# A graph-attention layer with gated residual and layernorm: reworked prologue, VectorE's own products in batch 0, x plus one moved on ScalarE

## What is computed

```python
h = einsum('bnd,ade->bane', x, W)            # features, per head
th = tanh(h)
attn = th @ w_src + swapaxes(th @ w_dst)     # 512 x 512 scores per head
attn = leaky_relu(attn, 0.2); attn = where(adj, attn, -999); attn = softmax(attn)
f = elu(concat(attn @ h + b))
gate = sigmoid(x @ H_w.T + H_b)
out = layernorm(x + gate * f + (1 - gate) * x)
```

## Time and profile before

| | us |
|---|---|
| median of 3 runs | 749.0 (747.43 to 750.62) |
| the profiled execution | 748.52 |
| its span | 746.7 |
| PE busy | 684.6 (92%) |
| DVE busy | 691.3 (93%) |
| ACT busy | 377.5 (51%) |
| POOL busy | 596.5 (80%) |

### The profile page before, as it was taken

How to read it: one execution, slowest core, us unless ns; L and a number is a source line. 1 busy time by engine, 2 the same in 40 slices (tenths; PEclk the granted TensorE clock), 3 DMA queues, 4 the chain that set the end, 5 groups by cost and what they waited for, 6 DMA issues and landing times.

```text
span 746.7 us, 12632 instructions
## 1 busy us (share of the span) xinstructions
PE 684.6 (92%) x3411; PEld 395.1 (53%) x3472; DVE 691.3 (93%) x1281; ACT 377.5 (51%) x804; POOL 596.5 (80%) x437
## 2 busy tenths in 40 slices
PE   4399999999999999999999999999999999999970
PEld 4355555555565555656555565655646465563430
DVE  8779999999999999999999999999999999999876
ACT  5123537374564637456473746547274654727161
POOL 6884697998979798897979889797988989793500
PEclk9599999999999999999999999999999999999995
DMA  5300111113121111212111121211211131111102
GB/s 184 99 1 2 57 43 43 58 43 100 44 98 42 45 58 47 89 42 98 42 55 60 51 73 42 98 42 69 64 49 57 42 98 42 57 43 43 42 2 84
DMA packets 32875, 43.82 MB, mean 59 GB/s; under 512 B 1234, under 2 KB 26580, under 8 KB 32852
## 3 DMA queue, kind: packets, MB, share of 16 engines
q1 hardware_dynamic: 24660, 31.35, 13.5%
q10 hardware_dynamic: 8192, 12.19, 4.5%
HBM read 30.95 MB, written 12.58 MB: 58 GB/s over the span
## 4 chain that ended last, share of the span: by engine, by line
PE 72%; DVE 17%; issue 5%; ACT 3%; DMA 2%; DVEq 1%; SPq 0%; POOL 0%; ACTq 0%; POOLq 0%
PE out_T L826 37%; PE hg L750 24%; DVE ew L610 9%; PE tr L834 5%; PE vb L812 4%; DVE ex L645 2%; PE hg L797 1%; DVE sd L559 1%; DMA ew<-in_HwT 1%; DVE th_w L541 1%; ACT x_plus L415 1%; PE hg L802 1%; DVE att L628 1%; ACT h_sb L381 1%; DVE ex L704 1%
## 5 line engine op out<-in xcount | busy, mean ns | idle before, releaser
L610 DVE SCALAR_TENSOR_TENSOR ew<-vb,u,adj_in 128x512 f32<-128x512 f32 x768 | 533.0, 737 | 2.3 <-PE vb L812 2.3
L826 PE MATMUL out_T<-ew,vals 128*64 128x512 f32 x1536 | 360.0, 600 | 3.3 <-DVE ew L610 1.3
L826 PEld LDWEIGHTS out_T<-ew,vals 128*64 128x64 f32 x1536 | 110.0, 136 | 194.5 <-issue 161.3
L258 POOL TENSOR_TENSOR th_w<-th,score_w 128x768 f32<-128x768 f32 x60 | 110.1, 1835 | 67.2 <-ACT th L380 61.6
L410 ACT ACTIVATE att_T<-out_T,tiny 128x512 f32<-128x512 f32 x96 | 66.1, 688 | 163.2 <-PE out_T L826 163.1
L750 PE MATMUL hg<-w_hi,xT_hi 128*128 128x384 f32 x384 | 109.7, 394 | 19.3 <-ACT xT_hi L371 7.7
L750 PE MATMUL hg<-w_hi,xT_lo 128*128 128x384 f32 x384 | 88.6, 338 | 0.3 <-DVE xT_lo L526 0.3
L750 PE MATMUL hg<-w_lo,xT_hi 128*128 128x384 f32 x384 | 88.2, 337 | 0.0
L750 PEld LDWEIGHTS hg<-w_hi,xT_hi 128*128 128x128 f32 x384 | 70.3, 194 | 27.2 <-issue 23.3
L262 POOL TENSOR_TENSOR th_w<-th_w 128x384 f32<-128x384 f32 x60 | 80.2, 1337 | 4.7
L387 ACT ACTIVATE gate_tanh<-hg 128x384 f32<-128x384 f32 x64 | 31.4, 490 | 95.7 <-PE hg L750 95.7
(11 more groups left out here) (97 smaller groups left out, 759.6 us busy)
## 6 DMA issues: line engine op xcount, KB each, us to landing
xT_in<-in_xT SPq DMA_DIRECT2D x16, 768.0 KB, 4.6
x_in<-in_x SPq DMA_DIRECT2D x16, 768.0 KB, 4.5
out<-y ACTq DMA_DIRECT2D x15, 768.0 KB, 3.5
adj_in<-in_adjT SPq DMA_DIRECT2D x16, 256.0 KB, 4.8
ew<-in_W SPq DMA_DIRECT2D x1, 576.0 KB, 4.2
ew<-in_HwT SPq DMA_DIRECT2D x1, 576.0 KB, 8.1
score_w<-in_w_rows SPq DMA_DIRECT2D x1, 384.0 KB, 7.1
out<-y SPq DMA_DIRECT2D x1, 384.0 KB, 2.5
```

The source lines that it names most:

```text
L258: g.tensor_tensor(th_w[:, c % 2], th[:, c].unsqueeze(1).broadcast_to([P, 2, D]), score_w[:], ALU.mult).then_inc(S["thw_done"], 1)
L610: ve.scalar_tensor_tensor(out=ew[:, (2 * C * j + i) % SLOTS, :], in0=VB[h % 4][:], scalar=u[:, q, c, h:h + 1], in1=adj_in[:, q, c, :], op0 ...
L826: te.matmul(OUT[VW * k:VW * k + VW, :], vals[:, q, c, h, :], ew[:, t % SLOTS, :], start=(c == 0), stop=(c == C - 1)).then_inc(S["ew_free"], 1)
```

## The change

- The gate weights are loaded into a buffer of their own. Their high part (ScalarE) is made after `copy_vT(0, 0)`, their low part (VectorE, `gate_low`) within batch 0's second head pair. The gate bias is split by ScalarE and GpSimd instead of VectorE.
- `head_sel` is built as a 12-wide `row_sel` by GpSimd and widened by one ScalarE copy.
- GpSimd adds batch 0's bias only after the column maximum, and makes only two of the four low splits of batch 1 before the values, the other two after the row sums.
- For batch 1, VectorE makes the score products of chunks 0 and 1 itself (`head_products`) and sums them 768 wide; GpSimd weighs only chunks 2 and 3.
- Batch 1's feature blocks alternate between the two banks. ScalarE's copy of a block of batch 1 waits for the values of its chunk and for the row sum, its tanh no longer does. The first attention matmuls wait for the values chunk by chunk.
- TensorE gets 58 matmuls without use for the result (`warm_up`), into the bank TR: 12 before the features, 16 after, 4 and 24 around the maximum's broadcast, 2 before the first `vb`.
- In every step ScalarE does x plus one behind the second feature block instead of in front of the first.

```diff
                 return HG[(c + 1) % 2]
+            if isinstance(b, int) and b == 1:
+                return HG[c % 2]
             return HG[1] if c == 3 else HG[0]
...
                 sp.dma_start(bias_row[:], bias.rearrange("(o n) -> o n", o=1).broadcast_to([P, E])).then_inc(S["ld_rows"], 16)
-                sp.dma_start(w_in[:, :, D:2 * D], HwT.rearrange("(k p) n -> p k n", p=P)).then_inc(S["ld_wg"], 16)
+                sp.dma_start(w_gate_in, HwT.rearrange("(k p) n -> p k n", p=P)).then_inc(S["ld_wg"], 16)
                 sp.wait_ge(S["pool_setup"], 1)
...
                 g.sem_inc(S["mixed"], 3)
+                g.sem_inc(S["thh_done"], 2)
                 g.memset(gate_bias_in[:], 0.0).then_inc(S["pool_setup"], 1)
...
                 g.memset(ident_bf[:], 0.0).then_inc(S["pool_setup"], 1)
-                g.memset(head_sel[:], 0.0).then_inc(S["pool_setup"], 1)
+                g.memset(row_sel[:], 0.0).then_inc(S["pool_setup"], 1)
                 g.memset(mean_w[:], 1.0 / N).then_inc(S["pool_setup"], 1)
...
                 for k in range(NPART):
-                    g.affine_select(out=head_sel[:], in_=head_sel[:], compare_op=ALU.not_equal, fill=1.0,
-                                    base=-H * k, pattern=[[-1, H], [0, P]],
-                                    channel_multiplier=1).then_inc(S["pool_setup"], 1)
+                    g.affine_select(out=row_sel[:], in_=row_sel[:], compare_op=ALU.not_equal, fill=1.0,
+                                    base=-H * k, pattern=[[-1, H]], channel_multiplier=1).then_inc(S["pool_setup"], 1)
                     pool.wait_ge(S["pool_setup"], 15 + k)
+                g.memset(vals[:, 1], 0.0).then_inc(S["pool_setup"], 1)
                 pool.wait_ge(S["ld_rows"], 16)
                 g.tensor_scalar(bias_row[:], bias_row[:], 1.0, 1.0, ALU.mult, ALU.add).then_inc(S["pool_setup"], 1)
-                g.memset(vals[:, 1], 0.0).then_inc(S["pool_setup"], 1)
                 pool.wait_ge(S["pool_setup"], SETUP)
+
+                pool.wait_ge(S["scores"], 1)
                 add_bias(0)
-                for c in range(C):
+                for c in range(2):
                     split_low(1, 1, c)
...
                 add_rows(0, 0)
+                for c in range(2, C):
+                    split_low(1, 1, c)
+                pool.wait_ge(S["gate_bias_split"], 2)
+                g.tensor_tensor(gate_bias[:], gate_bias_in[:], gate_bias_off, ALU.subtract).then_inc(S["gate_bias_done"], 1)
...
                 pool.wait_ge(S["th_done"], C * b + c + 1)
+                if isinstance(b, int) and b == 1:
+                    pool.wait_ge(S["thw_done"], C + c)
                 if c > 1 or not isinstance(b, int) or b:
...
                 if not last:
-                    for c in range(C):
+                    for c in range(2 if first else 0, C):
                         weigh(b + 1, c)
...
                 act.wait_ge(S["ld_w"], 16)
-                a.activation(w_hi[:, :, 0:D], w_in[:, :, 0:D], ACT.Copy).then_inc(S["w_hi_done"], 1)
+                a.activation(w_hi[:, :, 0:D], w_in, ACT.Copy).then_inc(S["w_hi_done"], 1)
                 for c in range(C):
                     split(0, 0, c)
-                act.wait_ge(S["ld_wg"], 16)
-                a.activation(w_hi[:, :, D:2 * D], w_in[:, :, D:2 * D], ACT.Copy).then_inc(S["w_hi_done"], 1)
                 for c in range(C):
...
                     split(1, 1, c)
+                act.wait_ge(S["pool_setup"], SETUP)
+                a.activation(head_sel[:], row_sel[:].unsqueeze(2).broadcast_to([P, H, P]), ACT.Copy).then_inc(S["head_sel_done"], 1)
                 act.wait_ge(S["dve_setup"], DVE_SETUP)
+                act.wait_ge(S["ld_hb"], 16 * 2)
+                a.activation(gate_bias_hi.bitcast(F32R), gate_bias_in[:], ACT.Copy).then_inc(S["gate_bias_split"], 1)
+                act.wait_ge(S["gate_bias_split"], 1)
+                a.activation(gate_bias_off, gate_bias_hi, ACT.Copy, scale=low_row[:, 0:1]).then_inc(S["gate_bias_split"], 1)
                 exps(0, 0)
                 copy_vT(0, 0)
+                act.wait_ge(S["ld_wg"], 16)
+                a.activation(w_hi[:, :, D:2 * D], w_gate_in, ACT.Copy).then_inc(S["w_hi_done"], 1)
...
                 act.wait_ge(S["h_done"], C * b + c + 1)
-                act.wait_ge(S["vals_done"], C * b)
-                if isinstance(b, int) and b == 1:
-                    act.wait_ge(S["hb_sum_done"], 1)
+                if not isinstance(b, int) or b > 1:
+                    act.wait_ge(S["vals_done"], C * b)
                 if not isinstance(b, int) or b:
...
                 a.activation(th[:, c], feature_bank(b, c)[:, 0:D], ACT.Tanh).then_inc(S["th_done"], 1)
+                if isinstance(b, int) and b == 1:
+                    act.wait_ge(S["vals_done"], c + 1)
+                    act.wait_ge(S["hb_sum_done"], 1)
                 a.activation(h_sb[:, c], feature_bank(b, c)[:, 0:D], ACT.Copy).then_inc(S["hcopy_done"], 1)
...
             def step(b, q, first, last, ahead=True):
-                if not first:
-                    x_forms(b - 1)
                 if not last:
...
                     features(b + 1, 1)
+                if not first:
+                    x_forms(b - 1)
                 copy_out(b, 0)
...
                                      ALU.subtract).then_inc(S["xlo_done"], 1)
-                dve.wait_ge(S["ld_wg"], 16)
-                dve.wait_ge(S["w_hi_done"], 2)
-                ve.tensor_tensor(w_lo[:, :, D:2 * D], w_in[:, :, D:2 * D], w_hi[:, :, D:2 * D].bitcast(F32),
-                                 ALU.subtract).then_inc(S["w_lo_done"], 1)
-                dve.wait_ge(S["ld_hb"], 16 * 2)
-                ve.tensor_copy(gate_bias[:], gate_bias_in[:]).then_inc(S["dve_setup"], 1)
-                dve.wait_ge(S["dve_setup"], 11)
-                ve.tensor_tensor(gate_bias[32:33, :], gate_bias_in[32:33, :], gate_bias[32:33, :].bitcast(F32),
-                                 ALU.subtract).then_inc(S["dve_setup"], 1)
                 dve.wait_ge(S["dve_setup"], DVE_SETUP)
+                dve.wait_ge(S["w_lo_done"], 1)
                 dve.wait_ge(S["ld_cols"], 16)
                 for c in range(C):
-                    dve.wait_ge(S["th_done"], c + 1)
-                    ve.tensor_tensor(th_w[:, c % 2], th[:, c].unsqueeze(1).broadcast_to([P, 2, D]), score_w[:],
-                                     ALU.mult).then_inc(S["thw_done"], 1)
+                    head_products(0, c)
                     head_sums(0, c)
...
+            def head_products(b, c):
+                dve.wait_ge(S["th_done"], C * b + c + 1)
+                if b:
+                    dve.wait_ge(S["sd_done"], C * b + c - 1)
+                ve.tensor_tensor(th_w[:, c % 2], th[:, c].unsqueeze(1).broadcast_to([P, 2, D]), score_w[:],
+                                 ALU.mult).then_inc(S["thw_done"], 1)
+
+            def gate_low():
+                dve.wait_ge(S["w_hi_done"], 2)
+                ve.tensor_tensor(w_lo[:, :, D:2 * D], w_gate_in, w_hi[:, :, D:2 * D].bitcast(F32),
+                                 ALU.subtract).then_inc(S["w_lo_done"], 1)
+
             def head_sums(b, c):
-                if isinstance(b, int) and b == 0:
-                    dve.wait_ge(S["thw_done"], c + 1)
+                if isinstance(b, int) and (b == 0 or b == 1 and c < 2):
+                    dve.wait_ge(S["thw_done"], C * b + c + 1)
                     t = th_w[:, c % 2].rearrange("p s (h e) -> p (s h) e", e=E)
...
                         between[8] = [lambda: head_sums(b + 1, 1)]
+                    if j == 1 and first:
+                        between[2] = [lambda: head_products(1, 0)] + between[2] + [gate_low]
+                        between[8] = [lambda: head_products(1, 1)] + between[8]
                     if j == 1 and not first:
...
                 te.sem_inc(S["ew_free"], SLOTS)
+                pe.wait_ge(S["dve_setup"], 3)
+                warm_up(WARM, v_parts[:, 0], v_parts[:].rearrange("p c n -> p (c n)"))
                 pe.wait_ge(S["w_hi_done"], 1)
...
                 pe.wait_ge(S["pool_setup"], SETUP)
+                pe.wait_ge(S["dve_setup"], DVE_SETUP)
+                warm_up(WARM + 4, v_parts[:, 0], v_parts[:].rearrange("p c n -> p (c n)"))
                 max_T(0)
+                warm_up(4, ident_bf[:], ident_bf[:])
                 max_all(0)
-                pe.wait_ge(S["w_lo_done"], 2)
-                pe.wait_ge(S["dve_setup"], DVE_SETUP)
+                warm_up(2 * WARM, ident_bf[:], ident_bf[:])
                 transpose_v(0)
+                pe.wait_ge(S["head_sel_done"], 1)
+                warm_up(2, ident_bf[:], head_sel[:, 0:4].rearrange("p h n -> p (h n)"))
                 broadcast_v(0, 0, 0)
                 broadcast_v(0, 0, 1)
+
+            def warm_up(n, l, r):
+
+                for _ in range(n):
+                    te.matmul(TR[:, 0:r.shape[1]], l, r, start=True, stop=True)
...
-                if c == 0:
```

(21 more changed lines are left out.)

13 lines of the change are left out of this document (8 added, 5 removed).

## The result

| | us |
|---|---|
| median after (4 runs) | 737.36 (736.72 to 738.14) |
| median before, same chip (4 runs) | 748.34 (747.43 to 750.62) |
| ratio after to before | 0.985 (0.983 to 0.987) |
| the profiled execution, its span | 738.14, 736.3 |
| PE, DVE, ACT, POOL busy | 694.9, 688.7, 382.0, 586.6 |

What follows compares the result with a forecast made beforehand. TensorE was taken to bound the steady part, VectorE within 2%. Prologue 8.9, batch 0 1.7 and steady part 3.6 sum to 14.2 us off 748.5: 734.3, forecast as a median of 735, range 730 to 741.

Steps and rivals of the forecast that it cites:

- Start of the products: Prologue: VectorE's first score product of batch 0 would start at about 9.9 us instead of 14.6.
- the clock is not held: Rival: fillers fail to keep TensorE's clock up in prologue and batch 1's first block; at most 6.8 us, 738.5; chance 0.10.
- The score weights were not late: Rival, prologue: score weights' transfer lands 3 us later than near 9, products start no sooner; 738; chance 0.03.
- the way to the first edge: Prologue, column maximum to first edge instruction: 0.9 us saved of 5.96, 0.1 us lost to ScalarE's added work.
- Batch 0: First batch: TensorE gains 2.4 us, VectorE gets 4.1 us more work; 41.3 us instead of 43.0, 1.7 gained.
- 0.2 us of holding up for each: Batch 0: GpSimd delays each of three added VectorE instructions by 0.2 us, as they begin near a GpSimd piece's end.
- The rival with a whole GpSimd instruction ahead of each: Batch 0: three added VectorE instructions each wait for a whole GpSimd one, 4.4 us less 0.6 counted; 738.8; chance 0.09.
- The steady part: Fourteen later batches: moving ScalarE's x plus one lets at most 0.26 us a batch through, 3.6 us in all.
- the tanh could have started near 293.6: Steady batch, ScalarE: the next batch's first-block tanh started at 293.89; moving x plus one saves 0.28 us.
- the steady part gave something: Against the rival that the steady part gives nothing: 738.5; chance 0.14.
- the wait of 0.67 us did not vanish: Against the rival that TensorE's whole steady-batch wait for ScalarE's copy goes: 5.7 us more gained, 729.3; chance 0.08.
- `att_T` was not late: Against the rival that x plus one delays `att_T` by 2.3 us in steady batches: slower, 756; chance 0.02.

Runs made afterwards that it cites:

- e4_xold: The changed kernel with x plus one put back in front of the first feature block's tanh in every step; 739.49 us.
- e8_own1: The changed kernel with VectorE making only chunk 0's product of batch 1 and GpSimd weighing chunk 1 as well; 736.01 us.
- e2_nofill: The changed kernel with all 58 added matmuls (five `warm_up` calls) taken out; 739.54 us.

## Why the prediction was right, and where its sizes were off

The forecast was 735.0 in a range of 730 to 741; 737.36 came. The mechanisms that it named were found at their places, with one exception: in the profiled execution the leading fillers did not hold the clock. Three terms were mis-sized, all too large: 14.2 us were forecast in all and the traces show 10.3. That the median is only 2.4 us off is in part luck. The sum gave 734.3 for an execution like the profiled one, which took 738.14, 3.8 more; the median happened to lie 0.8 below it, where 0.5 above was reckoned.

*Start of the products, 9.9 forecast, 11.63 measured.* The step that failed is "the twelve added matmuls run from about 1.3 us on, so I take the high level". Twelve at 0.43 us or less are over at 6.5 or earlier, so a pause before 7.7 was to be seen, and the earlier trace rows had shown a clock that fell within a pause of 4.4 us; I asked only whether the fillers raise it, not whether they reach the work. Where it held, the marks nearly come out: e4_xold has its first product at 10.26, its maximum at 17.80 (forecast 17.5) and its first edge at 22.82 (forecast 22.6). So 1.4 us at the first edge are a part of the case "the clock is not held" (6.8 in all), and 0.2 to 0.4 are left, because the sum had too little time between the ninth matmul and the first product. The score weights were not late, and the length of the products (7.54 for 7.6) and the way to the first edge (5.03 for 5.16) were right.

*Batch 0, 1.7 forecast, 0.8 measured.* The step is "0.2 us of holding up for each" added VectorE instruction. The gate weights' low part lost 0.77 us (2.13 against 1.36), since it began near the start of a split (the second of the two began at 32.7) and not near its end as the walk had it; the products lost 0.10 and nothing. And the added work held up GpSimd in turn: its first split was late by 0.7 us, which the walk left out. e8_own1 agrees that VectorE's added work bounded the batch in part: 1.35 us less of it gives 0.56. The rival with a whole GpSimd instruction ahead of each has the right mechanism, and it happened once in three, for most of a split. Its price was read too high: the 5.28 us for four splits, 1.3 each, were themselves stretched beside VectorE's fourth product (1.72 us there instead of 0.96), and undisturbed two take 1.97.

*The steady part, 0.26 a batch forecast, 0.16 to 0.20 measured.* The 43.27 us that the forecast starts from are a third of a stretch cut; by the means a batch took 43.21. The step that failed is "the tanh could have started near 293.6", 0.2 us behind the start of the transposes. It starts 0.29 behind it (284.61, 284.90) where it was 0.49, so 0.20 was to be had, and TensorE's wait fell by 0.17. That x plus one would just fit ahead of `att_T` was right to a tenth: 0.20 us are left of 1.65.

*The fillers.* The sixteen were said to be through at 17.4. They end near 19.2, where the maximum starts, because they started at 15.55 with the late first block: 0.0 us were left instead of 0.1. They held nothing up, since TensorE still waited 0.28 us for the maximum's end. As a whole the 58 are worth 2.2 us (e2_nofill).

None of the other rivals happened: the steady part gave something, the wait of 0.67 us did not vanish, `att_T` was not late.
